# A padded one-hot array, a merged VectorE operation, a clear shared with ScalarE and a step moved ahead, in the edge sort and first edge phase of a graph kernel

## The reference

```
h = xn @ Win.T + b_in
for l in range(3):                                   # three layers of messages
    Q, K, V = (h @ W.T + b).reshape(-1, 4, 64)       # per node, 4 heads
    attn = softmax(Q[src] . K[tgt] / 8)              # 4 x 4 per edge, over the heads of the target
    msg  = attn @ V[tgt] + Eemb[type]
    h    = relu(layer_norm(h + segment_sum(msg @ Wo.T + bo, src)))
x = x + xn + relu(h @ W1.T + b1) @ W2.T + b2
x = x + experts(layer_norm(x))                       # 8 experts, 2 per token, GELU, 256 -> 1024 -> 256
```

## Time and profile before

| | |
|---|---|
| median of 3 runs | 3538.44 us |
| the profiled execution | 3541.01 us, span 3539.2 us, mean granted TensorE clock 0.978 |
| busy, of the span | TensorE 3271.6 us (92%), its weight loads 2776.6 (78%), VectorE 2490.4 (70%), ScalarE 2416.9 (68%), GpSimd 2371.5 (67%) |
| instructions | 82,782 |

### The profile page before, as it was taken

The page is one execution under the profiler, slowest core; times in us unless marked ns, Lnnn a source line. Parts: engine busy times, 40 slices in busy tenths (PEclk is TensorE's granted clock), DMA queues, the critical chain, the costliest instruction groups (busy, mean ns, idle before and its releaser), DMA issues.

```text
span 3539.2 us, 82782 instructions
## 1 busy us (share of the span) xinstructions
PE 3271.6 (92%) x24455; PEld 2776.6 (78%) x24456; DVE 2490.4 (70%) x7379; ACT 2416.9 (68%) x5342; POOL 2371.5 (67%) x2552
## 2 busy tenths in 40 slices
PE   6999969999999898999999989999999998779998
PEld 3555459888888767888888876888888886679998
DVE  9888878788777756877777774777777788821111
ACT  3677658778777667877777756777777774334443
POOL 3656667777777757777777775777777776534443
PEclk9999979999999999999999999999999999889999
DMA  2111067777777537777777744777777775366664
GB/s 83 40 43 40 30 202 212 211 212 212 212 211 211 150 132 221 211 212 211 211 211 211 212 131 146 212 211 212 211 212 212 211 211 179 118 187 181 186 184 113
DMA packets 264839, 621.15 MB, mean 176 GB/s; under 512 B 85199, under 2 KB 129158, under 8 KB 256391
## 3 DMA queue, kind: packets, MB, share of 16 engines
q0 software_dynamic: 161376, 477.59, 48.5%
q1 hardware_dynamic: 103351, 142.22, 12.2%
HBM read 570.22 MB, written 49.62 MB: 175 GB/s over the span
## 4 chain that ended last, share of the span: by engine, by line
PE 42%; issue 19%; POOL 15%; DMA 14%; DVE 7%; ACT 1%; POOLq 1%; DVEq 0%; SPq 0%; ACTq 0%
POOL arena L607 15%; DMA arena<-kv_d,gidx 13%; PE bank L1743 7%; PE bank L1901 6%; PE bank L1913 5%; PE bank L1717 4%; PE bank L1732 3%; PE bank L1693 2%; PE bank L1589 2%; PE bank L1710 2%; PE bank L1660 2%; PE bank L1597 1%; PE bank L1687 1%; PE bank L1652 1%; PE bank L1658 1%
## 5 line engine op out<-in xcount | busy, mean ns | idle before, releaser
L607 POOL DMA_INDIRECT arena<-kv_d,gidx x1764 | 1683.7, 954 | 614.3 <-issue 529.9
L1743 PE MATMUL bank<-att,arena 128*128 128x128 f32 x7056 | 934.2, 276 | 15.7 <-DVE att L968 15.5
L1732 PE MATMUL bank<-qbd,kt_s 128*128 x7056 | 935.3, 276 | 0.3 <-ACT kt_s L1393 0.2
L1743 PEld LDWEIGHTS bank<-att,arena 128*128 128x128 f32 x7056 | 856.8, 192 | 21.1 <-DVE att L968 20.4
L1732 PEld LDWEIGHTS bank<-qbd,kt_s 128*128 128x128 f32 x7056 | 861.6, 193 | 1.1 <-issue 1.1
L939 DVE TENSOR_REDUCE sc<-bank 128x32 f32<-128x512 f32 x882 | 607.1, 688 | 314.1 <-PE bank L1732 301.2
L1717 PE MATMUL bank<-ident,arena 128*128 128x128 f32 x3528 | 684.2, 286 | 96.8 <-DMA arena<-kv_d,gidx 73.5
L1393 ACT ACTIVATE kt_s<-bank 128x512 f32<-128x512 f32 x882 | 525.0, 595 | 357.4 <-PE bank L1717 349.2
L1401 ACT ACTIVATE bank<-oh,bigc 128x512 f32<-128x512 bf16 x882 | 604.9, 686 | 47.7 <-PE bank L1765 22.7
L968 DVE TENSOR_TENSOR att<-bank,oh 128x512 f32<-128x512 f32 x882 | 601.9, 683 | 27.2 <-PE bank L1743 1.2
L1717 PEld LDWEIGHTS bank<-ident,arena 128*128 128x128 f32 x3528 | 403.6, 142 | 265.0 <-DMA arena<-kv_d,gidx 254.3
(11 more groups left out here) (248 smaller groups left out, 3863.2 us busy)
## 6 DMA issues: line engine op xcount, KB each, us to landing
arena<-in_pack SPq DMA_DIRECT2D x56, 1030.0 KB, 5.1
arena<-kv_d,gidx POOLq DMA_INDIRECT x1764, 3.7
kv_d<-arena SPq DMA_DIRECT2D x75, 256.0 KB, 2.0
hid_d<-arena SPq DMA_DIRECT2D x75, 128.0 KB, 2.0
xin<-hid_d SPq DMA_DIRECT2D x75, 128.0 KB, 2.1
arena<-in_w SPq DMA_DIRECT2D x8, 1024.0 KB, 8.3
oh<-oh_d SPq DMA_DIRECT2D x219, 32.0 KB
rec_d<-arena POOLq DMA_INDIRECT x241, 2.1
```

The source lines that it names most:

```text
L607: pool.indirect_dma_start(kv[:, t // UB, t % UB, :], None, kv_d, bass.IndirectOffsetOnAxis(gidx[:, h, t - h * HT:t - h * HT + 1], 0),).the ...
L1732: ins = mm(bk[:, :].rearrange("p (g t n) -> p t g n", g=H, t=2)[:, u, 2 * c:2 * c + 2], kt_s[:, p % 2, u, c, :], qbd[:, p // QP % 2, ds(w, ...
L1743: ins = mm(bank[6 + p // QP % 2][:, o:o + P], kv[:, b, u, D + g * DH:D + (g + 2) * DH], att[:, b % 2, u, :, g:g + 2, :].rearrange("p s g h ...
```

## The change

Four edits. (1) `oh_sy` gets rows of 64 columns instead of 48 and one row more per buffer, is cleared once, and L1660 takes two neighbouring rows as 128 weight columns, writing 128 rows of bank 2, of which 48 are read. (2) `code_of` makes both digits' codes by one `scalar_tensor_tensor` of 2 x 128 elements, five per chunk instead of ten. (3) `place` is written ahead of pieces 1 to 24 of `which`. (4) ScalarE clears 7472 columns of the sums in four activations (a copy scaled by 0) before its edge phase, after piece 0 of `which` and the stores of the input part; VectorE's pieces cover the 4736 columns of `oh_all` in five memsets and `rec_s` in a sixth. The counts of the semaphore for cleared sums move by one.

```diff
...
@@ -178,13 +179,13 @@
         early_b = early.bitcast(BF16)
-        n_win, n_sy = 2 * CH * NW, 2 * CH * SY
+        n_win, n_sy = 2 * CH * NW, 2 * (CH + 1) * SW
         late = arena[:, o_acc + n_oh:o_acc + 2 * n_oh]
         pe_code, pe_flag = late[:, 0:ET], late[:, ET:2 * ET]
         rec_code = late[:, 3 * ET:4 * ET].bitcast(I32)
         rec_in = arena[:, o_acc + 2 * n_oh - ET:o_acc + 2 * n_oh].bitcast(I32)
         oh_win = early_b[:, 0:n_win].rearrange("p (b k n) -> p b k n", b=2, k=CH)
-        oh_sy = early_b[:, n_win:n_win + n_sy].rearrange("p (b k n) -> p b k n", b=2, k=CH)
+        oh_sy = early_b[:, n_win:n_win + n_sy].rearrange("p (b k n) -> p b k n", b=2, k=CH + 1)
         qa_b = arena[:, o_qa:o_acc].bitcast(BF16)
@@ -197,6 +198,7 @@
         digits = [hi_f, wl_f]
+        both = arena[:, at_w + EC:at_w + EC + 2 * ECP].rearrange("p (k c) -> p k c", k=2)
         at_t = at_w + EC + 2 * ECP
@@ -726,6 +728,7 @@
             link(dve.memset(hi_f[:, EC:], float(HI)))
+            link(dve.memset(oh_sy[:, :, :, :], 0.0))
             link(dve.memset(wl_f[:, EC:], float(LO)))
@@ -769,7 +772,7 @@
                 dve.tensor_tensor(
-                    oh_sy[:, b, 0:n, :], iotab[:, 0:SY].unsqueeze(1).to_broadcast([P, n, SY]),
+                    oh_sy[:, b, 0:n, 0:SY], iotab[:, 0:SY].unsqueeze(1).to_broadcast([P, n, SY]),
                     sy_f[:, ds(k0, n)].unsqueeze(2).to_broadcast([P, n, SY]), ALU.is_equal)
@@ -780,16 +783,16 @@
 
-            def code_of(c, i):
-                j, k = i // 2, i % 2
+            def code_of(c, j):
                 e = c * CH + KS + j
-                if i == 0:
+                if j == 0:
                     dve.wait_ge(S.place_ready, c + 1)
                     if c >= 2:
                         dve.wait_ge(S.perm_used, c - 1)
-                ins = dve.tensor_scalar(coded[:, c % 2, j, k, :], iotab[:, 0:P], place_n[:, 0, c * MP + j:c * MP + j + 1],
-                                        digits[k][:, e:e + 1], ALU.is_equal, ALU.mult)
-                if i == 2 * MP - 1:
+                ins = dve.scalar_tensor_tensor(out=coded[:, c % 2, j], in0=iotab[:, 0:P].unsqueeze(1).to_broadcast([P, 2, P]),
+                                               scalar=place_n[:, 0, c * MP + j:c * MP + j + 1],
+                                               in1=both[:, :, e:e + 1].to_broadcast([P, 2, P]), op0=ALU.is_equal, op1=ALU.mult)
+                if j == MP - 1:
                     ins.then_inc(S.coded_ready, 1)
@@ -852,8 +855,8 @@
                     if c and n == CH:
-                        for i in range(2 * MP * k // CH, 2 * MP * (k + 1) // CH):
-                            code_of(c - 1, i)
+                        for j in range(MP * k // CH, MP * (k + 1) // CH):
+                            code_of(c - 1, j)
                     input_step(c, k)
@@ -876,8 +879,8 @@
                 slots(c, c % 2, c * CH, CH, CH if c < NCH - 1 else 1)
-            for i in range(2 * MP):
-                code_of(NCH - 1, i)
+            for j in range(MP):
+                code_of(NCH - 1, j)
             slots(NCH, 0, EF, 1, 0)
@@ -975,16 +978,13 @@
                         dve.wait_ge(S.oh_stored, NOB * 16)
-                        for j in range(G):
-                            dve.wait_ge(h_stored[j], IN)
-                            dve.wait_ge(kvo_stored[j], IN)
                         for k in range(TILES // TG):
                             dve.wait_ge(oh_landed[k], 16)
-                    n = n_qa // (AL - 1) // 8 * 8
-                    end = n_qa if c == AL - 2 else (c + 1) * n
-                    ins = dve.memset(arena[:, o_acc + c * n:o_acc + end], 0.0)
+                    n = n_oh // (AL - 2) // 8 * 8
                     if c == AL - 2:
-                        ins.then_inc(S.sums_zeroed, 1)
+                        dve.memset(rec_s, 0).then_inc(S.sums_zeroed, 1)
+                    else:
+                        dve.memset(arena[:, o_acc + c * n:o_acc + (n_oh if c == AL - 3 else (c + 1) * n)], 0.0)
 
@@ -1180,13 +1180,13 @@
                                 bank[5 + g % 3][0:ROWS, 0:2 * NW].rearrange("p (k w) -> p w k", k=2)).then_inc(S.cnt_copied, 1)
-            for c in range(1, NOH):
-                which(c)
             wreg = [dve.alloc_register(f"wv{u}") for u in range(TILES)]
             dve.wait_ge(S.ids_landed, 16)
             by_group = wid.rearrange("a (g t) -> a g t", t=QT)
             dve.tensor_tensor(place.rearrange("a (g t) -> a g t", t=QT), by_group,
                               by_group[:, :, 0:1].to_broadcast([1, NTURN * TILES // QT, QT]), ALU.subtract).then_inc(S.place_set, 1)
+            for c in range(1, NOH):
+                which(c)
             for l in range(L - 1):
@@ -1517,6 +1517,14 @@
                 indices(0, 0, h)
+            act.wait_ge(S.onehot_ready, 1)
+            for j in range(G):
+                act.wait_ge(h_stored[j], IN)
+                act.wait_ge(kvo_stored[j], IN)
+            for n0, n1 in ((n_oh, 2 * n_oh), (2 * n_oh + ET, n_qa)):
+                for a, b in ((n0, (n0 + n1) // 2), ((n0 + n1) // 2, n1)):
+                    ins = act.activation(arena[:, o_acc + a:o_acc + b], wt_one[:, 0:1].to_broadcast([P, b - a]), ACT.Copy, scale=0.0)
+            ins.then_inc(S.sums_zeroed, 1)
             areg = [act.alloc_register(f"wa{g}") for g in range(PAIRS // QP)]
@@ -1657,7 +1665,7 @@
                        start=False, stop=False, skip_group_check=True).then_inc(S.rank_ready, 1)
-                    mm(bank[2][0:SY, 2 * EX:2 * EX + NW], oh_sy[:, b, k, :], oh_win[:, b, k, :], start=False, stop=(n == 1), skip_group_check=True)
+                    mm(bank[2][:, 2 * EX:2 * EX + NW], oh_sy[:, b, k:k + 2, :].rearrange("p k n -> p (k n)"), oh_win[:, b, k, :], start=False, stop=(n == 1), skip_group_check=True)
                     if moved and k in MOVES:
...
```

More of the change, by code:

```diff
@@ L40 @@
 SY = 3 * W
+SW = 64
 REAL = 65536
@@ L643, in clear @@
                     pool.memset(acc[:, n * (P // W):(n + 1) * (P // W), :], 0.0).then_inc(S.sums_zeroed, 1)
-                    pool.wait_ge(S.sums_zeroed, 1 + l * NT + n + 1)
+                    pool.wait_ge(S.sums_zeroed, 2 + l * NT + n + 1)
                 for n in range(RA):
@@ L1028, in turn @@
                         if q == AL and first:
-                            dve.wait_ge(S.sums_zeroed, 1 + l * NT)
+                            dve.wait_ge(S.sums_zeroed, 2 + l * NT)
                         if q >= AL or not first:
```

## The result

The changed kernel takes 3485.51 us (median of 4 runs, 3484.29 to 3486.80) against 3537.84 us (4 runs) beside it: ratio 0.9854, interval 0.9837 to 0.9871, 52.3 us less. The forecast was 35.1 less, 3503, with a range from 3490: faster, as said, but outside the range. The profiled execution took 3484.9 us, its span 3482.8.

What follows compares the result with a forecast made beforehand. TensorE and VectorE taking turns were taken to set the sort's chunk, VectorE-bound after the edits; 30.3 us off the sort plus 4.8 behind it, 35.1 off 3538.4, gave 3503 us, range 3490 to 3521.

Steps and rivals of the forecast that it cites:

- TensorE's steps: Sort: TensorE's time per step from L1658 to the next L1652; its part of a chunk was to fall 1.83 us.
- where fp32 weights follow ... the kinds differ as they did, and I take nothing: Sort, behind L1660: no gain where the next load is fp32; the 0.19 us spacing stays.
- all gaps close: Rival, chance 0.14: fp32 loads behind L1660 hide as well, 12.07 us per chunk, 3493 us in all.
- VectorE's sum: Sort: VectorE's own work over a chunk's 13 steps, 11.24 us before and 11.20 with the edits.
- 0.20 in all 13 steps: Sort: upper bound on TensorE's gain per chunk from the wider weights, giving a chunk of 12.07 us.
- The merged operation: Sort, code_of: one instruction for two codes costs 0.39 us in a stream, saving 0.28 us of VectorE's work per chunk.
- The clearing of the padded array: Ahead of the sort's first chunk: 1792 more elements for VectorE to clear, costing 1.5 us on the path.
- half if 16-bit elements go two at a time: Alternative for clearing the padded array: half of the 1.5 us forecast.
- late next: Behind the sort: VectorE's first clear waits for the last one-hot store, leaving 1.5 of TensorE's 11 us gain.
- The width isn't the cause: Rival, chance 0.09: L1660 keeps its gaps despite 128 columns, 13.40 us per chunk, 3529 us in all.
- paid by its columns: Rival, chance 0.05: the wider load stays unhidden, 0.24 us in each of 13 steps, 3575 us in all.
- the merged operation is dear: Rival, chance 0.09: the instruction for two codes costs 0.57 us, 12.94 us per chunk, 3518 us in all.

Runs made afterwards that it cites:

- e1: Kernel before with only the padded one-hot array and 128 weight columns in the type product: 3487.93 us, ratio 0.9869.
- e2: Kernel before with only the merged operation making both digits' codes: 3528.95 us, ratio 0.9987.
- e13: Changed kernel with one VectorE wait for its own places, between them and the 24 one-hots: 3476.42 us, ratio 0.9850.
- e15: Changed kernel with the places moved ahead of the eight copies of the counts: 3475.87 us, ratio 0.9849.
- e7: Changed kernel with VectorE clearing all columns and no clear on ScalarE: 3480.82 us, ratio 0.9856.
- e6: Changed kernel with the places behind the 24 one-hots again: 3473.66 us, ratio 0.9838.
- e17: Kernel before with 96 weight columns in the type product (rows of 48, two neighbours): 3485.01 us, ratio 0.9873.

## Why the prediction was wrong

**TensorE's steps: the place right, the size wrong.** The step that failed is "where fp32 weights follow ... the kinds differ as they did, and I take nothing". The seven fp32 steps fell by more than the 0.09 in front: 1.33 to 1.05 for the key, value and projection steps, 0.92 to 0.64 for the queries, 0.65 to 0.39 for the transposes. The load behind the short one hides too (0.19 to 0.09), and the fp32 product itself is 0.08 shorter, which neither the forecast nor the rival "all gaps close" had. The permutations' steps went from 0.89 to 0.67, forecast 0.69. That the two engines take turns as the forecast stepped through them held: e1's chunk was worked out so before it ran, 11.8 us from the measured TensorE steps and VectorE's old ones, and 11.80 was measured. So the account held, and the term was mis-sized.

VectorE's sum has a slip beside it. Ten times 0.22 off 11.24 and five times 0.39 on make 10.99, not 11.20; 11.20 comes out if the three steps with nothing but a rank read are held at 0.36 us, and they take 0.29. With 10.99 the stepping gives some 12.26 with the forecast's TensorE steps, and 11.65 with the measured ones, as read; with 11.20 these give some 11.8. Chunks 4 to 26 took 267.5 us where they took 313.2 (from one L869, now L872, to another), 45.7 less, with 28.1 forecast. That is 17.6 of the sort's 21.4 us too little, some 14 of them TensorE's steps and 3 the slip; the chunks at either end gave 2.0 more than forecast, GpSimd's stall 1.0 and the clearing 0.8. The range had no room for TensorE's part since its bound, "0.20 in all 13 steps", was taken from gaps and left the product's own length out.

**The merged operation** was right: 0.48 alone and 0.40 spaced, forecast 0.39; e2's chunk of 13.39 is the 13.40 forecast for no gain on TensorE.

**The clearing of the padded array** cost about 0.7 us, not 1.5: the first chunk's places came at 47.04 instead of 46.33. The other bound, "half if 16-bit elements go two at a time", was the better one. **GpSimd** followed as said: idle 1.59 per chunk (forecast 1.9); the stall of 4.17 fell to 3.01.

**Behind the sort the step failed that lets TensorE go at 461.8 and has the first clear's wait for the store "late next".** It left out a wait: the gathers were taken to run beside the one-hots as in the kernel before, when the edit changes what VectorE executes right ahead of them, and one gather stood for 11.77 us. The clear's wait of some 5 us was right, though: e13 and e15 show it, 5.47 and 5.61, once the gather is free. In the changed kernel it is 1.28: there the last store lands 2.5 us behind the one-hots' end, in e13 6.7, and no gather but the standing one is under way beside it. That this is why was not tried. ScalarE's clear was hidden as said (done at 408.95, TensorE released at 409.88), but behind the late gather there was nothing for it to give (e7); with the places last it gave some 3 to 5 us (e6).

**The rivals.** "All gaps close" was the truth in the sort and still fell short, 3493 for 3485.5. "The width isn't the cause" and "paid by its columns" are refuted by e1 and e17, "the merged operation is dear" by e2.

## What to carry to other kernels

A stationary operand of few columns can cost more than one of 96 or 128, in the load, in the next load and in the next product: look at the idle time ahead of the load, not at its length, and try the wider one. Before an instruction is moved on VectorE, ask what it will run unbroken into, and who on GpSimd must get in between; one wait in such a run is cheap. When one wait is removed from the start of a phase that another engine paces, list every wait in that start, for the gain goes to the next one.

## What the runs showed of the hardware

- Loads of 48 and 64 bf16 columns were hidden neither in front nor behind (gaps of 0.18 and 0.20 us against 0.09), those of 96 and 128 were; an fp32 product behind a hidden one took 0.88 instead of 0.96 us.
- An int32 `tensor_tensor` of 600 elements on one partition, run unbroken into 24 `tensor_tensor` of 384 with two SBUF inputs, kept one GpSimd gather waiting for all of it, 11.8 to 12.4 us in six profiles, with a short reduction between in one of them. The same 24 without it ahead, or behind a wait, lengthened a gather by 0.15 to 0.29 us. The Trainium skill (SBUF — State Buffer, "Who interferes with whom") has the later of VectorE and GpSimd blocked for the whole of the other's instruction where both need the ports that they share. By that a gather would lose at most one one-hot, 0.5 us; e6 and e13 agree, while the changed kernel lost some 10.8, over 24 instructions. Why the places make that difference stays open.
